# A graph layer on one Trainium2 core: TensorE's counting as a loop, and its signals sent after a drain

## The chip, the cores and the metric

The kernel runs on one core of one Trainium2 chip. The metric is the time of one execution in microseconds (us) on the device. Lower is better.

## The reference, cut to what matters

The input is `x` (12500 nodes by 256 features), and 200000 edges `src[e] -> dst[e]`, sorted by `dst`. Two graph layers run over the same edges, each followed by a residual sum and a normalization:

```
out_deg = maximum(segment_sum(ones, src), 1)
t1  = x @ W1
msg = (t1[src] + x[src] * x[dst] @ W2) / sqrt(out_deg[src]) / sqrt(out_deg[dst])
embed = where(in_cnt > 0, t1 + segment_sum(msg, dst), 0) + b0
x = layernorm(x + l2norm(leaky_relu(embed)))
xt = x @ W.T + b1
x = layernorm(x + segment_sum(xt[src], dst) / (deg + 1))
```

## The kernel before

**What flows.** Edges stand in tiles of 128; there are 1568 of them with the padding, 32 to a round, 49 rounds to a layer. For each tile GpSimd issues one indirect DMA that gathers 128 rows of a table in DRAM (1 KB each) into one slot of a ring of 32 slots in SBUF (`ring`, line 478). TensorE multiplies the slot by a 0/1 matrix of the destinations that VectorE makes (`dst_hot`), 8 tiles to a group, so 4 groups to a round; the group's sum is in a PSUM bank, and VectorE adds it to the nodes' sums (`add_group`, line 850). The table is `scaled_x` in layer 0 (x times 1/sqrt of the out degree) and `x1`, layer 0's result, in layer 1.

**What a round does on TensorE** (`round_`, lines 1105 to 1130): for each group it waits for the destinations' matrix and the bank, for each tile for the gathered rows (`rows_in`), and issues one fp32 matmul of 128x257 (two MATMUL records in the profile). The group's last matmul increments `groups_done`. For that wait VectorE, which adds the group, and ScalarE, which then copies the source numbers of the same quarter of the next round into `idx` (`refill`, line 592); GpSimd waits for that (`idx_ready`) before it gathers the quarter. Between the tiles stand the previous round's nodes, two blocks of 128: `turn_halves` after tile 19 (transposes, `halves_turned`), `products` after tile 23 (matmuls with the weights, `projected`), and in layer 0 `find_places` after tile 7 (a look-up of scale factors, `places_found`). After the last round of a layer come one more `turn_halves` and `products`. Layer 1's gathers start only when all of layer 0's rows are stored (`table1_whole`, line 369).

**Kept rows.** In layer 0, the first 6 slots of 47 rounds are not gathered in the round. Their rows are gathered from `x` ahead of the layers, while the degrees are still being counted (282 gathers, `gather_kept`, line 488), stored in DRAM by SyncE (`store_kept`, line 327), loaded again in the round, and scaled by ScalarE (line 631).

**The counting of sources**, ahead of the layers. The out degree of each node is a histogram over 12544 bins, built as 128 x 98 in PSUM. 1120 tiles are counted by one-hot matrices of VectorE (line 695), 16 tiles to a batch, 70 batches (`SRC_BATCHES`), two buffers (`hot_made`, `hot_used`). The other 448 tiles are counted by ScalarE with Sign activations (line 554), which give step functions instead, 4 tiles to a batch, 112 batches (`STEP_BATCHES`), three buffers (`steps_made`, `steps_used`). ScalarE may write batch k only when TensorE has used batch k - 3:

```
act.wait_ge(steps_used, n + 1)        # starts at 3
```

TensorE multiplies both kinds, `hist_batch` 16 matmuls (line 1035) and `step_batch` 4 matmuls (line 1042), 128x98 in bf16. The order is written out: after hist batch n come the step batches from n*112//70 to (n+1)*112//70, one or two of them, so that the last two step batches follow the last hist batch. Then VectorE takes the differences of the step sums (lines 748 to 751, after `steps_used` has reached 115), TensorE adds them to the histogram (line 1060), ScalarE and VectorE make `r` = 1/sqrt(degree), scale x with it in 14 chunks (lines 571 and 761), and ScalarE's queue stores the chunks as `scaled_x` (line 576). GpSimd starts layer 0 when all kept rows are stored (line 498) and all 14 chunks are (line 501).

Of the kernel before, what the change touches and what calls it, by code (L numbers as in the profile page):

```python
# [24 lines left out]
P = 128  # L25
# [10 lines left out]
GT = 8  # L36
GR = U // GT
GROUPS = TILES // GT
DW = D + 1
# [10 lines left out]
STEP_BATCHES = 112  # L50
STEP_TILES = STEP_BATCHES * SB
SRC_BATCHES = (TILES - STEP_TILES) // HB
# [8 lines left out]
HOTS = 4  # L61
SUMS = 2
# [8 lines left out]
UNIT = 3  # L71
# [10 lines left out]
def gnn(nc, x, src, dst, w1, w2, b0, wl, b1, out):  # L82
# [6 lines left out]
    with ExitStack() as ctx:  # L89
# [10 lines left out]
        ring = sb("ring", [P, U, PITCH])  # L100
# [12 lines left out]
        place_hot = dst_col[:, 0:KE]  # L113
# [4 lines left out]
        dst_hot = hot_space  # L118
# [5 lines left out]
        halves = sb("halves", [P, 2, 2, D])  # L124
# [3 lines left out]
        ident = sb("ident", [P, P])  # L128
# [20 lines left out]
        r = sb("r", [P, NW])  # L149
# [25 lines left out]
        def group_sum(buf):  # L175
            return banks[:, buf, 0:DW]
# [3 lines left out]
        turned = [banks[:, 4 + s, :] for s in range(2)]  # L180
        project = [banks[:, 6, s * D:(s + 1) * D] for s in range(2)]
        found = banks[:, 2:4, 0:UNIT * NW].rearrange("p b (t n) -> p b t n", t=UNIT)
# [43 lines left out]
        places_found = sem("places_found")  # L226
# [13 lines left out]
        groups_done = sem("groups_done")  # L240
# [9 lines left out]
        halves_turned = sem("halves_turned")  # L250
        projected = sem("projected")
# [24 lines left out]
        def node_no(layer, m):  # L276

            return layer * ROUNDS + m
# [739 lines left out]
        def _(pe):  # L1018
# [13 lines left out]
            def hist_batch(n, half, first, last_one):  # L1032
                pe.wait_ge(hot_made, n + 1)
                for t in range(HB):
                    last = nc.tensor.matmul(hist, lo_hot[half][:, t, :], hi_hot[half][:, t, :],  # L1035
                                            start=first and t == 0, stop=last_one and t == HB - 1)
                last.then_inc(hot_used, 1)

            def step_batch(n, third, first, last_one):
                pe.wait_ge(steps_made, n + 1)  # L1040
                for t in range(SB):
                    last = nc.tensor.matmul(step_sums, steps[:, third, t, 0:P], steps[:, third, t, P:P + HI],  # L1042
                                            start=first and t == 0, stop=last_one and t == SB - 1)
                last.then_inc(steps_used, 1)
# [5 lines left out]
            for n in range(2):  # L1050
                last = nc.tensor.transpose(banks[0:BLOCKS, n, 0:P], bounds[:, n, :], ident[:, :])
            last.then_inc(bounds_turned, 1)

            pe.wait_ge(edges_in_cols, 2)
            for n in range(SRC_BATCHES):
                hist_batch(n, n % 2, n == 0, False)
                for k in range(n * STEP_BATCHES // SRC_BATCHES, (n + 1) * STEP_BATCHES // SRC_BATCHES):
                    step_batch(k, k % 3, k == 0, k == STEP_BATCHES - 1)
            pe.wait_ge(step_diffs_made, 1)
            nc.tensor.matmul(hist, between[:, :], step_rows[1], start=False, stop=True).then_inc(counts_whole, 1)  # L1060
            pe.wait_ge(bounds_read, 1)
# [1 line left out]
            for o, half in enumerate(wl_s):  # L1063
                for k in range(KF):
                    last = nc.tensor.transpose(banks[:, 0, k * D + o * P:k * D + (o + 1) * P], half[:, k, :], ident[:, :])
# [3 lines left out]
                             start=True, stop=True).then_inc(bad_summed, 1)  # L1069
            pe.wait_ge(bases_float, 1)  # L1070
            nc.tensor.matmul(banks[:, 7, P:P + GROUPS], ones[0:1, :], base_row_f[:, 0:GROUPS],
                             start=True, stop=True).then_inc(bases_spread, 1)

            def turn_halves(layer, m):

                for s in range(2):
                    if layer == 0:
                        pe.wait_ge(mixed, 2 * m + s + 1)
                    elif s == 0:
                        pe.wait_ge(sums_taken, m + 1)  # L1080
                    for h in range(2 if layer == 0 else 1):
                        for k in range(KF):
                            place = (h * KF + k) * P
                            last = nc.tensor.transpose(turned[s][:, place:place + P], halves[:, s, h, k * P:(k + 1) * P],  # L1084
                                                       ident[:, :])
                    last.then_inc(halves_turned, 1)

            def products(layer, m):

                weights = (w1_s, w2_s) if layer == 0 else (wt_s,)  # L1090
                for s in range(2):
                    pe.wait_ge(a_ready[s], node_no(layer, m) + 1)
                    parts = [(a_t[s][:, h, k, :], w[:, k, :]) for h, w in enumerate(weights) for k in range(KF)]
                    for n, (left, right) in enumerate(parts):
                        last = nc.tensor.matmul(project[s], left, right, start=n == 0, stop=n == len(parts) - 1)  # L1095
                    last.then_inc(projected, 1)

            def find_places(i):

                pe.wait_ge(places_made, i)  # L1100
                for t in range(KEPT):
                    last = nc.tensor.matmul(found[:, t // UNIT, t % UNIT, :], place_hot[:, t * P:(t + 1) * P], r[:, :],
                                            start=True, stop=True)
                last.then_inc(places_found, 1)

            def round_(layer, i, finish, end=U, with_kept=False, find=False):

                for k in range(GR):
                    pe.wait_ge(dst_hot_made, group_no(layer, i, k) + 1)
                    pe.wait_ge(groups_added, group_no(layer, i, k) + 1)  # L1110
                    tiles = range(k * GT, min((k + 1) * GT, end))
                    for u in tiles:
                        if with_kept and u < KEPT:
                            pe.wait_ge(kept_scaled, i)
                        elif u < KEPT:
                            rounds_before = (layer * 2 + i) if layer else (0 if isinstance(i, int) and i == 0 else 1)
                            pe.wait_ge(rows_in[u], 16 * (rounds_before + 1))
                        else:
                            rounds_before = layer * (ROUNDS if u < FINAL else ROUNDS - 1) + i
                            pe.wait_ge(rows_in[u], 16 * (rounds_before + 1))  # L1120
                        last = nc.tensor.matmul(group_sum(k % SUMS), dst_hot[:, k % HOTS, u - k * GT, :], ring[:, u, 0:DW],  # L1121
                                                start=u == tiles[0], stop=u == tiles[-1])
                        if u == tiles[-1]:
                            last.then_inc(groups_done, 1)
                        if find and u == FIND_U - 1:
                            find_places(i + 1)
                        if finish and u == TURN_U - 1:
                            turn_halves(layer, i - 1)
                        if finish and u == MIX_U - 1:
                            products(layer, i - 1)  # L1130
# [6 lines left out]
            with pe.If(disordered == 0):  # L1137
                for layer in range(2):
                    first = layer == 0
# [8 lines left out]
            with pe.Else():  # L1148
                for layer in range(2):
                    with pe.Fori(0, TILES) as t:  # L1150
                        n = layer * TILES + t
# [35 lines left out]
```

## Time and profile before

| | |
|---|---|
| median of 3 runs | 3994.8 us (3993.7 to 3995.43) |
| the profiled execution | 3996.79 us, its span 3995.1 us |
| busy: TensorE, its weight loads | 2991.8 us (75%), 1828.7 us (46%) |
| busy: VectorE, ScalarE, GpSimd | 1864.8 us (47%), 664.3 us (17%), 2982.0 us (75%) |
| counting of sources | 19.8 to 295 us |
| first gather of layer 0, of layer 1, end | 374.2, 2014.7, 3995.1 us |
| granted TensorE clock, mean | 0.748 |

The shares are averages over stages. A matmul's record has a modelled end. A pause of an engine is listed with what ended it.

### The profile page before, as it was taken

The page shows a single profiled execution, that of the slowest core. Times are in us where ns is not written, and L with a number is a line of the kernel's source. Part 1 is how long each engine was busy: PE and PEld are TensorE (multiplying, and loading weights), DVE is VectorE, ACT ScalarE, POOL GpSimd, SP SyncE. Part 2 cuts the span into 40 slices and gives each one's busy share as a digit, 9 for nine tenths or more (in the row PEclk, how much of TensorE's full clock was granted, in tenths as well). Part 3 has the DMA queues.
Part 4 walks back from the last instruction along what each step waited for, and adds up shares of the span by engine and source line. Part 5 has one row for each costly group of instructions (what it writes and reads, how often), then busy time and mean ns, then how long its engine had stood idle before and what let it go on. Part 6 is the DMA issues. An engine that isn't in the chain of part 4 may idle for free.

```text
span 3995.1 us, 42771 instructions
## 1 busy us (share of the span) xinstructions
PE 2991.8 (75%) x10186; PEld 1828.7 (46%) x10186; DVE 1864.8 (47%) x3536; ACT 664.3 (17%) x2054; POOL 2982.0 (75%) x3146
## 2 busy tenths in 40 slices
PE   4551777777777777777777877888888888878887
PEld 4441555555555555555433333344334343334443
DVE  9994555555555555555423333333333323232323
ACT  7992111111111111111100000000000000000000
POOL 7776777777777777777667777777777777777776
PEclk5555888988888888888867777666766666776667
DMA  8878455555555555555334443434443434343433
GB/s 256 272 233 309 150 156 155 155 156 155 156 155 155 156 158 156 158 155 156 116 94 118 117 118 116 119 115 120 115 120 115 120 115 120 115 121 114 120 115 107
DMA packets 294217, 582.43 MB, mean 146 GB/s; under 512 B 60723, under 2 KB 176100, under 8 KB 294180
## 3 DMA queue, kind: packets, MB, share of 16 engines
q0 software_dynamic: 150048, 409.93, 35.4%
q1 hardware_dynamic: 131364, 159.19, 11.9%
q10 hardware_dynamic: 12768, 12.85, 0.9%
q8 instruction: 20, 0.33, 0.0%
q14 instruction: 17, 0.14, 0.0%
HBM read 506.27 MB, written 75.45 MB: 146 GB/s over the span
## 4 chain that ended last, share of the span: by engine, by line
POOL 65%; issue 23%; POOLq 1%; PE 1%; DVE 0%; DVEq 0%; DMA 0%; ACT 0%; SPq 0%; ACTq 0%
POOL ring L478 65%; PE banks L1095 0%; POOLq L511 0%; DVEq L688 0%; POOLq L475 0%; PE banks L1121 0%; POOLq L476 0%; PE banks L1084 0%; DMA ring<-scaled_x,idx 0%; DMA ring<-x,idx 0%; POOL ring L488 0%; DMA x<-out_t 0%; DVE stats L917 0%; DVE out_t L929 0%; DVE big L850 0%
## 5 line engine op out<-in xcount | busy, mean ns | idle before, releaser
L1121 PE MATMUL banks<-ring,hot_space 128*128 128x257 f32 x6252 | 2470.7, 521 | 806.8 <-DMA ring<-x,idx 330.9
L1121 PEld LDWEIGHTS banks<-ring,hot_space 128*128 128x128 f32 x6252 | 1309.8, 242 | 1896.2 <-DMA ring<-x,idx 1058.0
L478 POOL DMA_INDIRECT ring<-x,idx x1563 | 1486.9, 951 | 505.3 <-issue 475.9
L478 POOL DMA_INDIRECT ring<-scaled_x,idx x1281 | 1221.2, 953 | 402.7 <-issue 402.7
L850 DVE SCALAR_TENSOR_TENSOR big<-banks,here_mask,big 128x257 f32 x784 | 343.9, 480 | 1604.5 <-PE banks L1121 1604.3
L806 DVE TENSOR_TENSOR hot_space<-banks,dst_rel 128x1024 f32<-128x1024 f32 x395 | 483.5, 1225 | 212.6 <-issue 210.8
L592 ACT COPY idx<-src_col 128x8 int32 (+1 forms) x392 | 77.3, 197 | 2145.7 <-PE banks L1121 2145.7
L488 POOL DMA_INDIRECT ring<-in_x,src_col x276 | 264.1, 957 | 84.1 <-issue 84.1
L554 ACT ACTIVATE dst_rel<-columns,halves 128x128 bf16<-128x128 f32 (+1 forms) x896 | 253.5, 374 | 23.8 <-PE banks L1042 19.6
L1035 PE MATMUL banks<-hot_space 128*128 128x98 bf16 x1120 | 104.2, 283 | 139.2 <-DVE hot_space L695 139.2
L1095 PE MATMUL banks<-w_s,a_t 128*128 128x256 f32 x784 | 179.3, 383 | 0.0
L1095 PEld LDWEIGHTS banks<-w_s,a_t 128*128 128x128 f32 x784 | 150.7, 192 | 20.8 <-ACT a_t L614 0.4
L1035 PEld LDWEIGHTS banks<-hot_space 128*128 128x128 bf16 x1120 | 89.2, 141 | 154.2 <-DVE hot_space L695 144.8
L695 DVE TENSOR_TENSOR hot_space<-banks,src_lo 128x2048 bf16<-128x2048 f32 x70 | 159.8, 2282 | 0.1
L695 DVE TENSOR_TENSOR hot_space<-banks,src_hi 128x1568 bf16<-128x1568 f32 x70 | 124.7, 1782 | 0.0
L614 ACT COPY a_t<-banks 128x512 f32<-128x512 f32 (+1 forms) x196 | 88.1, 480 | 219.5 <-PE banks L1084 219.0
L631 ACT ACTIVATE ring<-ring,r_kept 128x256 f32<-128x256 f32 x282 | 117.6, 495 | 22.4 <-issue 22.4
L1084 PE MATMUL banks<-ident,halves 128*128 128x128 f32 x588 | 108.6, 334 | 12.3 <-DVE halves L862 8.5
L1084 PEld LDWEIGHTS banks<-ident,halves 128*128 128x128 f32 x588 | 94.2, 178 | 34.4 <-DVE halves L862 10.8
L874 DVE SCALAR_TENSOR_TENSOR e<-banks,scal,b_s 128x256 f32<-128x256 f32 x98 | 42.9, 479 | 124.8 <-PE banks L1095 124.8
L1095 PE MATMUL banks<-wt_s,a_t 128*128 128x256 f32 x392 | 95.4, 388 | 0.1
L622 ACT ACTIVATE scal<-mv,epsilon 128x2 f32<-128x2 f32 x98 | 29.0, 295 | 370.2 <-DVEq L688 370.2
(115 smaller groups left out, 1193.2 us busy)
## 6 DMA issues: line engine op xcount, KB each, us to landing
kept_rows<-ring SPq DMA_DIRECT2D x94, 384.0 KB, 3.4
ring<-kept_rows SPq DMA_DIRECT2D x47, 768.0 KB, 5.5
ring<-x,idx POOLq DMA_INDIRECT x1563, 2.8
ring<-scaled_x,idx POOLq DMA_INDIRECT x1281, 2.8
dst_col<-in_src SPq DMA_DIRECT2D x47, 384.0 KB, 5.8
scaled_x<-big ACTq DMA_DIRECT2D x14, 896.0 KB, 17.5
x<-out_t SPq DMA_DIRECT2D x98, 128.0 KB, 2.4
x_t<-x SPq DMA_DIRECT2D x98, 128.0 KB, 2.3
```

The source lines that it names most:

```text
L478: g.indirect_dma_start(ring[:, u, 0:D], None, table[layer], bass.IndirectOffsetOnAxis(ap=idx[:, u:u + 1], axis=0)).then_inc(rows_in[u], 16)
L488: g.indirect_dma_start(early[place][:, t * D:(t + 1) * D], None, x, bass.IndirectOffsetOnAxis(ap=sources, axis=0)).then_inc(early_in[place ...
L554: last = nc.scalar.activation(steps[:, third, t, first:first + size], columns[:, 0:size], ACT.Sign, bias=step_digits[:, digit, bass.ds(n * ...
L614: nc.scalar.copy(a_t[s][:, 0:parts, :, :].rearrange("p h k n -> p (h k n)"), turned[s][:, 0:parts * D]).then_inc(a_ready[s], 1)
L631: last = nc.scalar.activation(ring[:, u, 0:D], ring[:, u, 0:D], ACT.Copy, scale=r_kept[:, bass.ds(i * KEPT + u, 1)])
L695: last = nc.vector.tensor_tensor(hots[half], lane_row[:, 0:size].unsqueeze(1).to_broadcast([P, HB, size]), vals.unsqueeze(2).to_broadcast( ...
L806: nc.vector.tensor_tensor(dst_hot[:, buf, :, :], lane_row.unsqueeze(1).to_broadcast([P, GT, P]), rel, ALU.is_equal).then_inc(dst_hot_made, 1)
L850: last = nc.vector.scalar_tensor_tensor(here, group_sum(k % SUMS), here_mask[:, n, bass.ds(i * GR + k, 1)], here, ALU.mult, ALU.add)
L1035: last = nc.tensor.matmul(hist, lo_hot[half][:, t, :], hi_hot[half][:, t, :], start=first and t == 0, stop=last_one and t == HB - 1)
L1084: last = nc.tensor.transpose(turned[s][:, place:place + P], halves[:, s, h, k * P:(k + 1) * P], ident[:, :])
L1095: last = nc.tensor.matmul(project[s], left, right, start=n == 0, stop=n == len(parts) - 1)
L1121: last = nc.tensor.matmul(group_sum(k % SUMS), dst_hot[:, k % HOTS, u - k * GT, :], ring[:, u, 0:DW], start=u == tiles[0], stop=u == tiles ...
```

## The change

It concerns TensorE's program alone. First, the counting is a loop. A "span" is two hist batches and three step batches: hist, step, step, hist, step. One span stands ahead of the loop and 34 in it, with waits on register values; 35 spans hold all 70 hist batches and 105 of the 112 step batches. The last 7 step batches stand behind the loop, one after the other. Second, in `turn_halves`, `products`, `find_places` and `round_` the increment no longer hangs on the last matmul: the engine drains and then increments by an instruction of its own.

```
-            for n in range(SRC_BATCHES):
-                hist_batch(n, n % 2, n == 0, False)
-                for k in range(n * STEP_BATCHES // SRC_BATCHES, (n + 1) * STEP_BATCHES // SRC_BATCHES):
-                    step_batch(k, k % 3, k == 0, k == STEP_BATCHES - 1)
+            def span(n, first):
+                for half in range(2):
+                    hist_batch(2 * n + half, half, first and half == 0, False)
+                    for third in ((0, 1), (2,))[half]:
+                        step_batch(3 * n + third, third, first and third == 0, False)
+
+            span(0, True)
+            with pe.Fori(1, SRC_BATCHES // 2) as n:
+                span(n, False)
+            for k in range(SRC_BATCHES // 2 * 3, STEP_BATCHES):
+                step_batch(k, k % 3, False, k == STEP_BATCHES - 1)
...
-                    last.then_inc(halves_turned, 1)
+                    pe.drain()
+                    pe.sem_inc(halves_turned, 1)
...
-                    last.then_inc(projected, 1)
+                    pe.drain()
+                    pe.sem_inc(projected, 1)
...
-                last.then_inc(places_found, 1)
+                pe.drain()
+                pe.sem_inc(places_found, 1)
...
                         if u == tiles[-1]:
-                            last.then_inc(groups_done, 1)
+                            pe.drain()
+                            pe.sem_inc(groups_done, 1)
```

How TensorE's instructions stand at the end of the counting, before (L1035 is a hist batch, L1042 a row of step batches at 4 matmuls each, L1060 adds the steps' differences, L1065 transposes a weight):

```order
L1035 MATMUL banks<-hot_space 128x98 x16
L1042 MATMUL banks<-dst_rel 128x98 x4
L1035 MATMUL banks<-hot_space 128x98 x16
L1042 MATMUL banks<-dst_rel 128x98 x8
L1035 MATMUL banks<-hot_space 128x98 x16
L1042 MATMUL banks<-dst_rel 128x98 x8
L1060 MATMUL banks<-e,between 128x98
L1065 MATMUL banks<-ident,a_t 128x128 x4
```

The same place now, from the loop's first row to the weight's transposes (`REGISTER_ALU` and `ISA` are the registers' work for the waits and the loop; L1068 and L1073 are what L1060 and L1065 were):

```order
L1035 MATMUL banks<-hot_space 128x98 x16
L1040 ISA
L1042 MATMUL banks<-dst_rel 128x98 x4
L1040 REGISTER_ALU
L1042 MATMUL banks<-dst_rel 128x98 x4
L1033 REGISTER_ALU
L1035 MATMUL banks<-hot_space 128x98 x16
L1040 REGISTER_ALU
L1042 MATMUL banks<-dst_rel 128x98 x4
L1063 REGISTER_ALU
L1063 COMPARE_AND_BRANCH
L1042 MATMUL banks<-dst_rel 128x98 x28
```

Where 2 step batches (8 matmuls) stood behind the last hist batch, 1 stands in the loop's last pass and 7 (28 matmuls) behind it. The order of the two layers' matmuls is the same as before; drains and increments have no row in these lists.

## Rows read from the trace of the kernel before

**Rows 1.** The page, chain that ended last, shares by engine.

```profile
POOL 65%; issue 23%; POOLq 1%; PE 1%; DVE 0%; DVEq 0%; DMA 0%; ACT 0%; SPq 0%; ACTq 0%
```

**Rows 2.** The page, groups: busy, mean ns, idle before.

```profile
L478 POOL DMA_INDIRECT ring<-scaled_x,idx x1281 | 1221.2, 953 | 402.7 <-issue 402.7
```

**Rows 3.** Windows, a layer each: PE, PEld, DVE, ACT, POOL busy, PEclk, DMA share, GB/s.

```profile
600.00:1800.00 1200.00, 895.01 (x3663) 678.80 (x3662) 690.68 (x1505) 201.81 (x552) 909.35 (x955) 0.88 0.51 156
2400.00:3600.00 1200.00, 995.74 (x2272) 479.61 (x2271) 376.84 (x778) 71.88 (x239) 909.08 (x956) 0.69 0.41 117
```

**Rows 4.** Waits in one round of layer 0, 1146 to 1178.6 us.

```profile
PE banks L1121 <- DMA ring<-scaled_x,idx: 4.6, 7, 1.2
PE banks L1121 <- ACT ring L631: 3.5, 1, 3.5
```

**Rows 5.** Timeline of ScalarE: the second refill of a round.

```profile
1151.63 0.20 ACT L592 COPY idx<-src_col 128x8 int32 x1 [6.04 <-PE banks L1121]
```

**Rows 6.** Timeline of TensorE: 8 tiles in a row, one tile alone.

```profile
1179.95 3.66 PE L1121 MATMUL banks<-ring,hot_space 128*128 128x257 f32 x16
1184.54 0.67 PE L1121 MATMUL banks<-ring,hot_space 128*128 128x257 f32 x2 [0.93 <-DMA ring<-scaled_x,idx]
```

**Rows 7.** The page, DMA issues: count, median us to landing.

```profile
ring<-scaled_x,idx POOLq DMA_INDIRECT x1281, 2.8
```

**Rows 8.** Chain between counting and layer 0: start us, us, what.

```profile
361.45 10.44 issue
371.89 0.04 POOLq L501
```

**Rows 9.** Timeline of ScalarE at the same place.

```profile
370.90 1.69 ACT L585 COPY big<-zeros 128x1792 f32<-128x1792 f32 x1 [1.65 <-DMA scaled_x<-big]
```

**Rows 10.** Timeline of both layers' ends.

```profile
1987.66 0.88 DVE L874 SCALAR_TENSOR_TENSOR e<-banks,scal,b_s 128x256 f32<-128x256 f32 x2 [2.56 <-PE banks L1095]
...
2005.12 0.88 DVE L874 SCALAR_TENSOR_TENSOR e<-banks,scal,b_s 128x256 f32<-128x256 f32 x2 [7.09 <-PE banks L1095]
...
2014.68 0.94 POOL L478 DMA_INDIRECT ring<-x,idx  x1 [29.41 <-SPq L369]
...
3989.07 0.88 DVE L900 SCALAR_TENSOR_TENSOR out_t<-banks,scal,e 128x256 f32<-128x256 f32 x2 [1.20 <-PE banks L1095]
```

**Rows 11.** Timeline of 283 to 295 us, the counting's end.

```profile
283.02 6.82 ACT L554 ACTIVATE dst_rel<-columns,halves 128x128 bf16<-128x128 f32 x24 [0.41 <-PE banks L1042]
...
290.07 0.86 PE L1042 MATMUL banks<-dst_rel 128*128 128x98 bf16 x8
...
290.74 2.34 ACT L554 ACTIVATE dst_rel<-columns,halves 128x128 bf16<-128x128 f32 x8 [0.90 <-PE banks L1042]
...
292.68 1.49 PE L1035 MATMUL banks<-hot_space 128*128 128x98 bf16 x16 [1.75 <-DVE hot_space L695]
...
293.97 0.85 PE L1042 MATMUL banks<-dst_rel 128*128 128x98 bf16 x8
...
294.86 0.26 DVE L748 COPY e<-banks 128x98 f32<-128x98 f32 x1 [1.65 <-PE banks L1042]
```

**Rows 12.** Waits of 2400 to 3600 us: TensorE's pauses without a releaser.

```profile
PEld banks L1121 <- issue: 52.0, 59, 1.2
```

**Rows 13.** Timeline of ScalarE's queue: the first store of scaled_x.

```profile
304.38 0.39 ACTq L576 DMA_DIRECT2D scaled_x<-big  x1
```

**Rows 14.** DMA queues, 304 to 361.5 us: packets, MB, share of 16 engines.

```profile
q10 hardware_dynamic: 11379, 11.46, 57.7%
q0 software_dynamic: 1992, 5.47, 23.8%
q1 hardware_dynamic: 1916, 5.16, 23.7%
```

**Rows 15.** DMA queues, 361.5 to 372 us.

```profile
q10 hardware_dynamic: 1389, 1.39, 37.5%
```

**Rows 16.** Timeline of TensorE: 8 tiles in a row at the lower clock.

```profile
420.27 6.70 PE L1121 MATMUL banks<-ring,hot_space 128*128 128x257 f32 x16 [3.21 <-ACT ring L631]
```

More of the change, by code:

```diff
@@ L1083, in turn_halves @@
                             place = (h * KF + k) * P
-                            last = nc.tensor.transpose(turned[s][:, place:place + P], halves[:, s, h, k * P:(k + 1) * P],
-                                                       ident[:, :])
-                    last.then_inc(halves_turned, 1)
+                            nc.tensor.transpose(turned[s][:, place:place + P], halves[:, s, h, k * P:(k + 1) * P],
+                                                ident[:, :])
+                    pe.drain()
+                    pe.sem_inc(halves_turned, 1)
             def products(layer, m):
@@ L1094, in products @@
                     for n, (left, right) in enumerate(parts):
-                        last = nc.tensor.matmul(project[s], left, right, start=n == 0, stop=n == len(parts) - 1)
-                    last.then_inc(projected, 1)
+                        nc.tensor.matmul(project[s], left, right, start=n == 0, stop=n == len(parts) - 1)
+                    pe.drain()
+                    pe.sem_inc(projected, 1)
             def find_places(i):
@@ L1101, in find_places @@
                 for t in range(KEPT):
-                    last = nc.tensor.matmul(found[:, t // UNIT, t % UNIT, :], place_hot[:, t * P:(t + 1) * P], r[:, :],
+                    nc.tensor.matmul(found[:, t // UNIT, t % UNIT, :], place_hot[:, t * P:(t + 1) * P], r[:, :],
                                             start=True, stop=True)
-                last.then_inc(places_found, 1)
+                pe.drain()
+                pe.sem_inc(places_found, 1)
             def round_(layer, i, finish, end=U, with_kept=False, find=False):
@@ L1120, in round_ @@
                             pe.wait_ge(rows_in[u], 16 * (rounds_before + 1))
-                        last = nc.tensor.matmul(group_sum(k % SUMS), dst_hot[:, k % HOTS, u - k * GT, :], ring[:, u, 0:DW],
+                        nc.tensor.matmul(group_sum(k % SUMS), dst_hot[:, k % HOTS, u - k * GT, :], ring[:, u, 0:DW],
                                                 start=u == tiles[0], stop=u == tiles[-1])
                         if u == tiles[-1]:
-                            last.then_inc(groups_done, 1)
+                            pe.drain()
+                            pe.sem_inc(groups_done, 1)
                         if find and u == FIND_U - 1:
```

## The prediction

> **What bounds the kernel now.** I read first the chain that ended last. It is GpSimd with 65% and "issue" with 23% [rows 1], and the groups say what that is, in layer 0 1281 gathers of 0.953 us with 402.7/1281 = 0.31 us before each [rows 2], so one gather each 1.26 us. The reader should see that the pause before a gather has no releaser other than issue: in the rounds GpSimd waits for nobody. Then the windows: in 1200 us GpSimd is busy 909 us in either layer, while TensorE has 895 us in layer 0 and 996 us in layer 1 [rows 3]. TensorE is the second load, not the bound. The waits of one round of layer 0 say what it has in hand: of 32.6 us (26 gathers) it waits 4.6 us for gathered rows and 3.5 us for ScalarE's scaling [rows 4], 8.1 us together. A late TensorE reaches GpSimd only through `idx`, and there is more room: ScalarE refilled the round's second quarter at 1151.8 us [rows 5], while TensorE waited for tile 16 until 1184.5 us [rows 6], 2.8 us after its gather was issued [rows 7]. Tile 16 was thus issued at about 1181.7 us and tile 8, the first of that quarter, eight gathers earlier, at about 1171.7 us: 20 us of room.
>
> So the end is set where GpSimd does wait, and at the two ends of layers. Between counting and layer 0 it waits 10.44 us, until 371.89 us [rows 8]. The last chunk of `scaled_x` had landed by 370.9 us, when ScalarE starts to zero its place [rows 9], so the last 1.0 us belongs to the last kept store. At the end of layer 0 it waits 29.41 us for the stored rows [rows 10], and behind the last gather of layer 1 stands a similar tail.
>
> **The loop.** Its registers and branch come to six rows for two hist batches. TensorE waits 1.75 us for VectorE before a hist batch [rows 11], and VectorE has a second buffer; the bound from above for a turn of a loop is the 1.2 us that is the longest pause without a releaser in the rounds, which are a loop already [rows 12]. It is hidden: 0 us. Should a turn cost over 1.75 us, the second buffer is next to cover it.
>
> The step batches are what changes. A span uses 3 for 2 hist batches, before it was 3.2. ScalarE makes one in 6.82/3 = 2.27 us when nothing holds it [rows 11], and a span has two periods of VectorE, 2 x 3.9 = 7.8 us (292.68 less 288.78), for 3 x 2.27 = 6.8 us. It was held by the buffers already (0.41 and 0.90 us before its last pieces); now it is held more, and cannot use the time to run ahead by more than three. Now the end. Before, ScalarE starts the last step batch at 290.74 us, when TensorE has freed a buffer behind the last but one hist batch, and TensorE is done with all at 293.97 + 0.85 = 294.82 us [rows 11]. In the changed order the same moment frees the buffer for step batch 105, and behind it stand 105 to 111, seven batches: 290.74 + 7 x 2.27 = 306.6, and TensorE's four matmuls 0.4 to 0.5 us more, 307.1 us. The counting ends **12.3 us later**.
>
> What that costs: `r`, the scaling and the stores of `scaled_x` all shift; the first store was issued at 304.38 us [rows 13] and goes to 316.7 us. But the stores are bound by the DMA engines and shared with the kept rows, whose gathers end at 361.45 us as before. From 304.38 to 361.5 us the stores' queue q10 moved 11.46 MB, 0.201 MB a us, beside 5.47 and 5.16 MB of the two others [rows 14], and 1.39 MB were left for the time after [rows 15]. With the later start it moves 44.8 x 0.201 = 9.0 MB by then and leaves 3.86 MB, 2.47 MB more. GpSimd issues no gathers after 361.45 us, so the engines are the stores': all three queues together moved 22.1 MB in 57.5 us, 0.384 MB a us, and q10 alone had 57.7% of the engines for its 11.46 MB, which is 0.345 at 100%. 2.47 MB take 6.4 us by the one, 7.2 us by the other. I take 6.6: the last chunk lands at 377.5 instead of 370.9 us, GpSimd goes on at 377.5 instead of 371.9, **+5.6 us**. Bounds: 0 (the 1.0 us of slack and full cover) and +11.3 (no cover: 370.9 + 12.3).
>
> "Issuing engines are not separate DMA queues" in the Trainium skill's page DMA: Bandwidth & Descriptors says that transfers of all queues run on the same 16 engines and interleave; by it the stores take over what the gathers leave, as taken here. The rows agree so far that the three queues' shares sum to about 105% of the engines.
>
> **The drains.** Each round has 4 for groups, 2 for transposes, 2 for products, in layer 0 also one for the look-up: 9 and 8. No drain of TensorE is in the trace. Nearest is the difference between tiles in a row, 3.66/8 = 0.46 us, and a tile alone, 0.67 us [rows 6]: 0.21 us to fill and empty, which a drain exposes when work stands behind it. The drain and the increment are queue instructions; one such on GpSimd takes 0.04 us [rows 8], two 0.08. So 0.3 us where TensorE has work behind it, 0.1 us on a signal alone. From below 0; from above nothing shows it, and I use twice, 0.6.
>
> In the rounds: 9 x 0.3 = 2.7 us against 8.1 us of waiting, and behind that the 20 us of `idx`. Hidden, 0 us. Without that cover it would be 47 x 2.7 = 127 us. In the tails they lie on the path. Layer 0's last round, up to VectorE's work at 1987.66 us [rows 10]: two transposes' drains, a group's, the first product's, 4 x 0.3, and the last product's signal, 0.1: 1.3 us. Then up to 2005.12 us [rows 10] one 0.3 and one 0.1; the transposes' are covered by ScalarE's clearing of the sums. Layer 1, up to 3989.07 us [rows 10]: a group's signal, a transposes' signal, and 0.3 + 0.1 for products, 0.6. Sum **2.3 us**, bounds 0 and 5.
>
> The Trainium skill's page TensorE: Matmul & The Clock Gate, "Single matmul latency", gives about 175 ns by which a lone matmul exceeds its columns' time, and in "Step-by-step" that a stream hides it; this speaks against the change, and the 0.21 us of the rows are near it. By its figure the sum of the tails would be an estimated 2.1 us.
>
> **Sum.** 5.6 + 2.3 = 7.9 us. The profiled execution took 3996.79 us, 1.7 above its span and 2.0 above the median of 3994.8; it would come to 4004.7, the median to 4002.7. A measurement of this kernel can tell 0.2% or 8.0 us from no change, so this forecast lies just inside the bound, as a small loss.
>
> **The rivals.**
>
> *Slower, the stores don't speed up.* If q10 keeps its 0.201 MB a us after the gathers end, 3.86 MB take 19.2 us: 380.7, +8.8 us; with the tails +11.1, 4005.9 us. With no cover at all +11.3 + 2.3, 4008.4. It decides from a rate under about 0.33 MB a us. For it: a queue alone at full rate is nowhere in the trace. Against: q10's share of 57.7% grows when others stop.
>
> *Hidden.* The last step batches come sooner than I have them, or the kept stores end the wait in any case; only the tails are left: +2.3, 3997.1 us. For it: 1.0 us of slack is there. Against: 12.3 us is far more than that.
>
> *Slower, dear drains.* If a drain costs more than 8.1/9 = 0.9 us, TensorE can't follow in layer 0: at 1.0 us it is 9 x 0.1 x 46 = 41 us more, 4044 us. Against: a tile alone ends after 0.67 us in all.
>
> *Slower, the clock.* The granted clock was 0.88 in layer 0, so about a quarter of the time at 1.2 GHz [rows 3]. At that level 8 tiles take 6.70 us [rows 16] against 3.66 [rows 6], 32 tiles 26.8 against 14.6 us. If drains kept it there, a round's tiles alone would grow by 12.2 us, over the 8.1 in hand: 4 us x 46 = +190, 4190 us. Against: a TensorE that falls behind no longer waits for rows, and the clock comes back; GpSimd sets how much it has to do in a us. The page of the clock gate says in "HAM oscillation" that pauses between bursts throttle the engine, which is this rival's mechanism.
>
> **How the numbers follow.** Forecast 0.60; stores that don't speed up 0.20; hidden 0.12; drains 0.03 and clock 0.03; faster for a reason I don't see 0.02. The forecast's own range is 3999.5 to 4006, and since its middle is at the bound, I give 0.25 of its 0.60 to slower. Slower: 0.25 + 0.20 + 0.06 = 0.51; faster 0.03; within 0.46. The range: from 3997 (hidden) to 4012 (no cover, tails at their upper bound).
>
> **What would show it.** Step batches at the counting's end: 7 pieces of 4 matmuls, 2.27 us apart, to 307 us. First gather of layer 0 at 379.8 instead of 374.2. Rounds of 32.6 and 40.2 us as before, GpSimd's pauses 0.3 us. Pauses of 0.2 to 0.3 us on TensorE behind products and transposes. From layer 0's last gather to layer 1's first 1.7 us more, and 0.6 at the end. It is wrong if GpSimd waits within a round, if the first gather moves by under 3 or over 8 us, or if layers change their length by more than 3 us.

## The result and the profile after

The changed kernel takes **4011.52 us** (median of 6 runs, 4010.28 to 4013.43) against 3995.01 us of the kernel before in as many runs beside it. The ratio is 1.0041 (95% interval 1.0031 to 1.0051), so it is slower by 16.5 us. The profiled spans are 4010.5 and 3995.1 us, 15.4 us apart, and this is where they part:

| stretch | before, us | after, us | difference |
|---|---|---|---|
| start to the first gather of layer 0 | 374.2 | 380.1 | +5.9 |
| first to last gather of layer 0 | 1610.1 | 1621.6 | +11.5 |
| last gather of layer 0 to the first of layer 1 | 30.4 | 31.5 | +1.2 |
| first to last gather of layer 1 | 1961.8 | 1958.0 | -3.8 |
| last gather to the end | 18.6 | 19.2 | +0.7 |

**The start.** Timeline of the counting's end, TensorE, ScalarE and VectorE, of the changed kernel; it answers to [rows 11] and [rows 13]:

```profile
291.11 15.75 ACT L554 ACTIVATE dst_rel<-columns,halves 128x128 bf16<-128x128 f32 x56 [0.98 <-PE banks L1042]
...
304.68 0.51 PE L1042 MATMUL banks<-dst_rel 128*128 128x98 bf16 x4 [1.73 <-ACT dst_rel L554]
...
306.92 0.51 PE L1042 MATMUL banks<-dst_rel 128*128 128x98 bf16 x4 [1.73 <-ACT dst_rel L554]
307.46 0.26 DVE L748 COPY e<-banks 128x98 f32<-128x98 f32 x1 [13.94 <-PE banks L1042]
316.98 0.39 ACTq L576 DMA_DIRECT2D scaled_x<-big  x1
```

ScalarE makes its last 7 batches (56 activations, 8 to a batch) without a stop. TensorE takes one every 2.24 us and waits 1.73 us before each. VectorE goes on at 307.46 instead of 294.86 us, the first store is at 316.98 instead of 304.38: 12.6 us later, both. The first fence below has q10, the stores' queue, from 304 to 361.5 us (against [rows 14]: 11.46 MB), the second from 361.5 to 380 us (against [rows 15]: 1.39 MB); columns: packets, MB, share of 16 engines.

```profile
q10 hardware_dynamic: 8989, 9.05, 46.1%
```

```profile
q10 hardware_dynamic: 3779, 3.80, 59.1%
```

Chain that ended last, at the same place: the last store lands at 378.2 us, and GpSimd passes its wait; then the first gather on GpSimd's timeline (both answer to [rows 8]):

```profile
366.63 11.57 DMA scaled_x<-big
...
378.40 0.51 POOLq L503
```

```profile
380.08 0.94 POOL L478 DMA_INDIRECT ring<-scaled_x,idx  x1 [18.25 <-issue]
```

**The layers.** The page's groups of gathers (busy us, mean ns, idle before and its releaser):

```profile
L478 POOL DMA_INDIRECT ring<-x,idx x1563 | 1483.2, 949 | 506.4 <-issue 475.8
L478 POOL DMA_INDIRECT ring<-scaled_x,idx x1281 | 1232.7, 962 | 408.1 <-issue 407.5
```

Against [rows 2] the 1281 gathers of layer 0 are busy for 1232.7 instead of 1221.2 us. The idle time before them, less 12.76 and 18.25 us before the first, is 389.9 both times. In both profiles no pause before a gather within a layer is over 0.32 us. So GpSimd waits for nobody in the rounds, as before, and the 11.5 us are in the gathers' own length. In layer 1 they are shorter, 1483.2 against 1486.9 us. The windows (columns as in [rows 3]) show no slower TensorE clock, 0.90 and 0.74 against 0.88 and 0.69:

```profile
600.00:1800.00 1200.00, 927.01 (x3646) 665.34 (x3645) 686.63 (x1487) 198.47 (x545) 911.78 (x947) 0.90 0.51 155
2400.00:3600.00 1200.00, 943.64 (x2275) 463.72 (x2276) 379.41 (x775) 73.23 (x239) 908.50 (x958) 0.74 0.40 118
```

**What a drain costs TensorE.** Timeline of the changed kernel, TensorE's weight loads and matmuls of `products` in one round:

```profile
1169.77 1.59 PEld L1104 LDWEIGHTS banks<-w_s,a_t 128*128 128x128 f32 x8 [0.48 <-issue]
1169.78 4.06 PE L1104 MATMUL banks<-w_s,a_t 128*128 128x256 f32 x16
...
1171.84 1.59 PEld L1104 LDWEIGHTS banks<-w_s,a_t 128*128 128x128 f32 x8 [0.48 <-issue]
```

Each half's loads begin 0.48 us after the loads of the half before ended; between the two halves stand one drain and one increment. The whole piece took 3.62 us before and takes 4.06 (the median of 49 such pieces in either kernel).

**Layers' ends**, timeline, answering to [rows 10]:

```profile
2005.68 0.88 DVE L874 SCALAR_TENSOR_TENSOR e<-banks,scal,b_s 128x256 f32<-128x256 f32 x2 [3.25 <-PEq L1105]
...
2023.69 0.88 DVE L874 SCALAR_TENSOR_TENSOR e<-banks,scal,b_s 128x256 f32<-128x256 f32 x2 [7.65 <-PEq L1105]
...
2033.24 0.94 POOL L478 DMA_INDIRECT ring<-x,idx  x1 [30.61 <-SPq L369]
```

30.61 us between the layers against 29.41; with the 0.7 us at the end the tails cost 1.9 us.

**Why gathers got longer.** A plain gather takes 0.946 us. In layer 0, 72 of 1281 were over 0.962 us before and 171 are now; what they have over 0.946 sums to 10.1 and 21.2 us (counts and sums here and below are worked out from the trace's records of gathers and of VectorE's instructions). Here is one of them in the changed kernel, with VectorE beside it, and the same instruction of the kernel before, both from timelines:

```profile
1140.80 0.94 POOL L478 DMA_INDIRECT ring<-scaled_x,idx  x1 [0.30 <-issue]
1142.05 1.07 POOL L478 DMA_INDIRECT ring<-scaled_x,idx  x1 [0.30 <-issue]
```

```profile
1141.88 0.76 DVE L878 SCALAR_TENSOR_TENSOR e<-e 128x256 f32<-128x256 f32 x2
```

```profile
1162.97 0.95 POOL L478 DMA_INDIRECT ring<-scaled_x,idx  x1 [0.30 <-issue]
1164.23 0.95 POOL L478 DMA_INDIRECT ring<-scaled_x,idx  x1 [0.30 <-issue]
```

```profile
1163.38 0.76 DVE L878 SCALAR_TENSOR_TENSOR e<-e 128x256 f32<-128x256 f32 x2
```

After, the first of L878's two instructions of about 0.42 us is running when the gather at 1142.05 starts, and ends 0.25 us after that start; the gather takes 0.12 us more. Before, L878 lay between the starts of two gathers and both took 0.95. For 308 of the 351 long gathers of the two profiles, the surplus is what remains of VectorE's instruction at the gather's start, less 0.13 us, to within 0.01 us. Only some instructions do it: those with two inputs in SBUF (L860, L862, L878, L895, L913) and some with a single one in SBUF (L813, L815, L929, all three of them `TENSOR_SCALAR`). L850, L874 and L900, which read PSUM, run over gathers' starts and hold none; nor does L917, which has a single input in SBUF. Who began first matters as well: 50 times one of the holding lines, with over 0.15 us to go, had begun less than 0.12 us ahead of the gather, and the gather kept its length.

42 of the other 43 long gathers are lengthened in a second way. Here L806, which holds nobody, runs at the gather's start, and L813 begins 0.35 us behind it:

```profile
1151.39 1.22 DVE L806 TENSOR_TENSOR hot_space<-banks,dst_rel 128x1024 f32<-128x1024 f32 x1 [1.58 <-issue]
1152.18 1.01 POOL L478 DMA_INDIRECT ring<-scaled_x,idx  x1 [0.30 <-issue]
1152.53 0.55 DVE L813 TENSOR_SCALAR dst_col<-dst_col 128x768 int32<-128x768 int32 x1
```

The gather ends at 1153.19 us, 0.11 us after L813's end at 1153.08. All 42 look like this: L813 begins 0.31 to 0.37 us after the gather, and the gather ends 0.12 us after L813. There are 4 of them in the kernel before, for 0.3 us, and 38 in the changed one, for 2.2 us. So the step to 21.2 us is 5.7 us of L878, 2.9 us of L813 and L815 running at the start, 1.9 us of L813 begun later, and 0.6 us of L860 and L862.

So my theory for the rounds was: **a drain delays TensorE's signal, the signal moves VectorE's work by some tenths of a us against GpSimd's raster of 1.25 us, and more of it falls on the moments at which a gather can be held.** The rivals: late TensorE work reaches GpSimd in another way (through `idx`, or the order of the DMAs); or the loop has to do with it.

### The profile page after: what moved, and what is told of

Same layout as the page of the kernel before. It is cut to its first block, busy times and chain, and to the rows that moved or that the text cites. A ratio compares the mean times of both kernels' runs of the same rounds, so it can differ in the third digit from the quotient of the medians.

```text
span 4010.5 us, 43841 instructions
## 1 busy us (share of the span) xinstructions
PE 2967.2 (74%) x10186; PEld 1787.7 (45%) x10186; DVE 1871.8 (47%) x3536; ACT 665.3 (17%) x2054; POOL 2990.2 (75%) x3146
## 4 chain that ended last, share of the span: by engine, by line
POOL 64%; issue 24%; DVE 6%; ACTq 1%; DMA 1%; PEld 1%; POOLq 1%; ACT 1%; DVEq 1%; PEldq 0%; SPq 0%; PE 0%
POOL ring L478 64%; DVE hot_space L695 6%; ACTq L576 1%; PEld banks L1132 0%; DVEq L688 0%; DMA ring<-scaled_x,idx 0%; DMA scaled_x<-big 0%; POOLq L511 0%; ACT dst_rel L554 0%; PEldq L1135 0%; ACT big L571 0%; POOLq L475 0%; PEldq L1105 0%; PEld banks L1104 0%; DVEq L733 0%
## 5 line engine op out<-in xcount | busy, mean ns | idle before, releaser
L1132 PE MATMUL banks<-ring,hot_space 128*128 128x257 f32 x6252 | 2325.1, 504 | 796.2 <-DMA ring<-x,idx 356.9
L478 POOL DMA_INDIRECT ring<-x,idx x1563 | 1483.2, 949 | 506.4 <-issue 475.8
L478 POOL DMA_INDIRECT ring<-scaled_x,idx x1281 | 1232.7, 962 | 408.1 <-issue 407.5
L850 DVE SCALAR_TENSOR_TENSOR big<-banks,here_mask,big 128x257 f32 x784 | 343.6, 480 | 1564.6 <-PEq L1135 1564.6
L806 DVE TENSOR_TENSOR hot_space<-banks,dst_rel 128x1024 f32<-128x1024 f32 x395 | 483.4, 1224 | 216.6 <-issue 213.8
L1035 PE MATMUL banks<-hot_space 128*128 128x98 bf16 x1120 | 104.2, 282 | 141.2 <-DVE hot_space L695 141.2
L1104 PE MATMUL banks<-w_s,a_t 128*128 128x256 f32 x784 | 196.6, 394 | 7.9
L1104 PEld LDWEIGHTS banks<-w_s,a_t 128*128 128x128 f32 x784 | 141.9, 191 | 62.7 <-issue 46.6
L1035 PEld LDWEIGHTS banks<-hot_space 128*128 128x128 bf16 x1120 | 89.2, 141 | 156.2 <-DVE hot_space L695 146.8
L1092 PE MATMUL banks<-ident,halves 128*128 128x128 f32 x588 | 125.1, 329 | 25.5 <-DVE halves L862 10.2
L1104 PE MATMUL banks<-wt_s,a_t 128*128 128x256 f32 x392 | 114.2, 415 | 13.9 <-issue 9.7
L874 DVE SCALAR_TENSOR_TENSOR e<-banks,scal,b_s 128x256 f32<-128x256 f32 x98 | 42.9, 479 | 158.3 <-PEq L1105 158.3
L1092 PEld LDWEIGHTS banks<-ident,halves 128*128 128x128 f32 x588 | 82.2, 167 | 76.9 <-issue 43.0
L1104 PEld LDWEIGHTS banks<-wt_s,a_t 128*128 128x128 f32 x392 | 68.6, 195 | 62.8 <-issue 56.7
## 6 DMA issues: line engine op xcount, KB each, us to landing
scaled_x<-big ACTq DMA_DIRECT2D x14, 896.0 KB, 16.5
```

The costliest lines, as they stand in the source:

```text
L478: g.indirect_dma_start(ring[:, u, 0:D], None, table[layer], bass.IndirectOffsetOnAxis(ap=idx[:, u:u + 1], axis=0)).then_inc(rows_in[u], 16)
L806: nc.vector.tensor_tensor(dst_hot[:, buf, :, :], lane_row.unsqueeze(1).to_broadcast([P, GT, P]), rel, ALU.is_equal).then_inc(dst_hot_made, 1)
L850: last = nc.vector.scalar_tensor_tensor(here, group_sum(k % SUMS), here_mask[:, n, bass.ds(i * GR + k, 1)], here, ALU.mult, ALU.add)
```

## The experiments

Short diffs are against the kernel before unless another is named. The same counts for all profiled kernels: long gathers and their surplus in us, in layer 0 with the share of VectorE's lines (named by their numbers in the kernel before), and in layer 1. "L813 later" is the second way, L813 begun after the gather's start. The plain gather is 946 ns, in the rows with * 949.

| kernel | layer 0 | of it L813, L815 | L813 later | L860, L862 | L878 | L913 | layer 1 |
|---|---|---|---|---|---|---|---|
| before | 72, 10.1 | 3.2 | 0.3 | 5.7 | 0.6 | 0.2 | 69, 8.9 |
| changed | 171, 21.2 | 6.1 | 2.2 | 6.3 | 6.3 | under 0.2 | 39, 5.6 |
| changed, again* | 171, 20.6 | 6.5 | 2.1 | 5.4 | 6.3 | 0.2 | 41, 5.4 |
| drains alone | 158, 22.0 | 5.5 | 2.2 | 6.5 | 7.2 | 0.3 | 51, 6.9 |
| loop and order alone | 74, 9.9 | 2.5 | 0.2 | 6.1 | 0.8 | 0.4 | 69, 9.0 |
| order alone* | 83, 10.5 | 2.8 | 0.1 | 6.9 | under 0.2 | 0.3 | 67, 8.4 |
| drain in `products` alone | 130, 17.3 | 1.2 | 0.5 | 5.7 | 7.0 | 2.5 | 75, 9.0 |
| drains of groups alone | 141, 18.5 | 2.2 | 0.3 | 6.3 | 6.8 | 2.6 | 66, 9.6 |
| drain in `turn_halves` alone | 80, 11.0 | 2.2 | 0.3 | 6.8 | 0.8 | 0.5 | 53, 5.7 |
| drain in `find_places` alone* | 80, 10.3 | 2.4 | 0.4 | 6.8 | 0.3 | 0.2 | 63, 7.7 |
| changed, two copies ahead of L874 | 110, 11.3 | 0.9 | 0.2 | 5.3 | 2.5 | 2.3 | 45, 6.5 |
| changed, one copy | 107, 16.7 | 2.2 | 2.0 | 6.3 | 0.2 | under 0.2 | 51, 6.7 |
| before, bias in PSUM | 87, 11.0 | 3.6 | 0.4 | 5.9 | 0.7 | 0.3 | 8, 0.6 |
| changed, bias in PSUM | 165, 20.6 | 6.0 | 2.5 | 4.9 | 6.9 | 0.2 | 8, 0.6 |

### Drains alone, loop and order alone

Drains alone: all four drains, the counting as before.

```
-                    last.then_inc(projected, 1)
+                    pe.drain()
+                    pe.sem_inc(projected, 1)
```

and so in the three other places.

> The kernel before with all four kinds of drain and the counting unrolled in its old order. Theory A (collisions): the drains move VectorE's work against GpSimd's gathers, and gathers that coincide with certain VectorE instructions take longer; so this run has the changed kernel's gather time in layer 0, 1232.7 us busy against 1221.2, with no shift of the first gather: it starts at 374.2 us, and the kernel takes 9 to 11 us more than before, about 4005. Theory B (the later start does it: the counting moves something in time and the layers' gathers suffer from that): gathers stay at 1221 us, only the tails' 2 us are left, about 3997.

Loop and order alone: the first hunk of the change, and no drain.

> The changed kernel's counting alone, no drains. Theory A: first gather at 380.1 us, 5.9 later than before, gathers of layer 0 at about 1221 us busy, 4001 us in all. Theory B: first gather at 380.1 and gathers at about 1233 us, 4010 us.

Measured, beside 3996.94 us of the kernel before: drains alone 4008.75 (ratio 1.0028, 1.0018 to 1.0039), +11.8 us; loop and order 4002.73 (1.0015, 1.0005 to 1.0024), +5.8 us. Page of the drains alone, then of loop and order alone:

```profile
L478 POOL DMA_INDIRECT ring<-scaled_x,idx x1281 | 1233.6, 963 | 402.8 <-issue 401.6
```

```profile
L478 POOL DMA_INDIRECT ring<-scaled_x,idx x1281 | 1220.9, 953 | 408.0 <-issue 408.0
```

The first gather is at 374.30 us with the drains alone and at 379.79 with loop and order alone. The two parts add up within their intervals: 11.8 + 5.8 = 17.6 against 16.5 us for the change. With loop and order alone the gathers keep their 1220.9 us, so the loop has nothing to do with the rounds.

### Order alone

Against the changed kernel, with the drains undone too:

```
-            with pe.Fori(1, SRC_BATCHES // 2) as n:
+            for n in range(1, SRC_BATCHES // 2):
```

> The changed order of the counting, three step batches to two hist batches and seven at the end, written out without a loop, and no drains. If the order alone makes the delay: first gather at 379.8 to 380.1 us as with the loop, 7 pieces of step batches at the end. If the loop's turns or its register waits have a part in it: the first gather comes before 379 us.

One run, 4010.97 us, on a chip where the kernel before takes 4003.9 (19 runs). The first gather is at 380.37 us; in the one run with the drain in `find_places` alone, on the same chip, it is at 374.63: +5.7 us without any loop, against 374.2 to 379.8 with it. So the whole 5.7 to 5.9 us come with the order, that is the seven step batches at the end; the loop's registers and branches cost nothing that shows.

### One kind of drain at a time

Each of these has one of the four drains, in the kernel before.

> The kernel before with drains behind the products alone. Theory A: VectorE's L878 and L881, which follow the products, are most of the new collisions (1 and 6 of 94 gathers hit before, 43 and 88 in the changed kernel), while L813 and L815, which follow a group, are as before (4 and 23 of 47): about half of the 11.5 us, so 5 to 7 us, about 4001. If each kind only adds its own small delay and the collisions need all of them, under 2 us, 3997. Theory B: nothing, under 1 us.

> The kernel before with drains at the groups' ends alone. Theory A: L813, L815 and L819 move into the gathers (38, 41 and 45 hits of 47 in the changed kernel against 4, 23 and 25), L878 and L881 stay out of them: 3 to 6 us, about 4000. Theory B: under 1 us.

> The kernel before with a drain behind the transposes alone. Theory A: it delays the second block's transposes and the products by about 0.3 us or less, and VectorE's work on the products with them; L878 would start at 0.6 instead of 0.3 and 0.7 us after a gather's start, 1.0 for its second half, just ahead of the point where it holds the next gather. Layer 0's gathers 1 to 7 us over before's, less than with drains at the products or groups.

> The kernel before with a drain behind the look-up alone. Theory A: its signal is awaited by VectorE's L826, which stands between a group's matrices and its sum; it delays little, so layer 0's gathers are within 3 us of 1221 us busy.

| drain alone in | median, us | before beside it | ratio (95%) | gathers of layer 0, busy us |
|---|---|---|---|---|
| `products` | 4004.56 | 3996.94 | 1.0020 (1.0010 to 1.0029) | 1228.8 |
| groups | 4004.97 | 3996.94 | 1.0020 (1.0011 to 1.0030) | 1230.1 |
| `turn_halves` | 3993.63, one run | 3996.69 | | 1221.9 |
| `find_places` | 4004.83, one run | 4003.9 | | 1224.9 (plain 949) |

The four are not a sum: `products` and groups give 7.6 and 8.0 us each and all together 11.8. A cost of the drains themselves would add up. The table above fits with that: each of the two alone brings L878 onto gathers' starts (0.6 to 7.0 and 6.8 us), which can happen only once. I had looked for the groups' drains to show in L813 and L815, VectorE's work in front of a group; they didn't (3.2 before, 2.2). The groups' drains delay the products behind them as well, which would move the same L878, and L913 behind it; this link wasn't tested by itself. The 5.5 us of L813 and L815 come only with several drains together. For drains in `turn_halves` alone I had expected 1 to 7 us more in layer 0's gathers; the one run shows 0.7, no cost in all, and in layer 1 L895 partly off the starts (layer 1's surplus 8.9 to 5.7 us). For `find_places` the one run shows no cost either.

### Moving VectorE by hand

If only the position counts, more delay on the changed kernel should give time back. In `finish_sums`, layer 0, ahead of L874, two copies that nobody reads:

```
                     v.wait_ge(projected, 2 * m + 4)
+                    for n in (P, P // 8):
+                        nc.vector.tensor_copy(columns[:, 0:n], lane_row[:, 0:n])
+                        ordered()
```

> The changed kernel, with two small copies and drains, some 0.5 us of extra work, in VectorE's queue ahead of its work on layer 0's products (L874 and what follows). Nothing is left out. Theory A (a gather is held when it needs the port at about 0.1 us after its start while L878 runs): more work on VectorE puts L878 back between these moments, its about 44 held gathers in layer 0 fall below 10, and the gathers' busy time of layer 0 falls from 1232.7 us by 5 to 6 us, if the later work (L860 to L862, L813, L815) is not moved into them more than it is now; the kernel is faster than the changed one by 3 to 6 us. Rival C (TensorE's drains slow the gathers directly, or VectorE's load as such does): the gathers stay at 1232 us or get longer, 4011 us or more.

Timeline of VectorE: the copies delay the next instruction by 0.73 us.

```profile
1169.11 0.54 DVE L874 COPY columns<-banks 128x128 f32<-128x128 f32 x2 [3.13 <-PEq L1108]
1169.84 0.88 DVE L877 SCALAR_TENSOR_TENSOR e<-banks,scal,b_s 128x256 f32<-128x256 f32 x2 [0.19 <-issue]
```

Median 4012.3 us of 10 runs (4005.0 to 4015.58) beside 4003.9: ratio 1.0021 (1.0011 to 1.0030), where the change has 1.0041 (1.0031 to 1.0051), and in a second set of runs 1.0043 (1.0026 to 1.0060). The sets were not run side by side. Its page:

```profile
L478 POOL DMA_INDIRECT ring<-scaled_x,idx x1281 | 1222.6, 954 | 408.6 <-issue 405.2
```

The profiled execution is the quickest of the ten, 4005.0. The 3.4 us that "issue" leaves open are 11 of the usual pauses of 0.3 us, put down to `idx`; none is over 0.31 us. With more work on VectorE in every round, the gathers of layer 0 are 10.1 us shorter than in the changed kernel. A theory in which lateness costs time would have them longer. L878 was freed only in part, though: I had expected fewer than 10 held gathers, 20 were left, and L913 came to hold 40 for 2.3 us.

The same with one copy, 0.38 us, to see whether L878 alone can be moved, next to the changed kernel on the same chip:

```
+                    nc.vector.tensor_copy(columns[:, :], lane_row)
+                    ordered()
```

> The changed kernel with one copy and drain, some 0.45 us, in VectorE's queue ahead of its work on layer 0's products; the last try had two and moved L878 by 0.73 us, which freed L878 in half its cases and brought L913 into the gathers instead. Theory A: L878 stands 0.11 to 0.27 us after a gather's start in the changed kernel and 0.3 to 0.5 us in the one before, where it holds nobody; by 0.45 us later it is there again. Held gathers at L878 from 44 to under 5, L913's stay under 10, layer 0's gathers about 1226 us busy, 6 us faster than the changed kernel here. Rival C: more work on VectorE, no gain.

> The changed kernel, unaltered, on the same chip as the next two, since a comparison with it across chips is uncertain by some us. Gathers of layer 0 at 1232 us busy (or that much more than before by 11 us, if this chip's gathers all take some ns longer), 16 us slower than before.

One copy: 4008.79 us (5 runs; 1.0034, 1.0020 to 1.0048); the changed kernel again: 4013.45 us (4 runs; 1.0043, 1.0026 to 1.0060), beside 3996.69. The medians differ by 4.7 us and the surplus by 20.6 - 16.7 = 3.9, but the intervals overlap, so the times alone don't settle it. The records do: of the 6.3 us of L878, 0.2 are left, and L881 behind it, which held one gather for 0.1 us in the changed kernel, now holds 36 gathers for 5.7 us. The copy moved the clash by one instruction, which I had not expected. L815 lost 4.0 of its 6.0 us. This run also shows the clash from the other side, in 28 of the 47 rounds that have an L813:

```profile
658.69 0.95 POOL L478 DMA_INDIRECT ring<-scaled_x,idx  x1 [0.30 <-issue]
659.25 0.77 DVE L813 TENSOR_SCALAR dst_col<-dst_col 128x768 int32<-128x768 int32 x1
```

L813, begun 0.54 to 0.60 us after the gather, takes 0.73 to 0.79 instead of 0.55 us, and the gather keeps its 0.95. Begun 0.34 to 0.53 us after the gather (13 times in this run), L813 keeps its length and the gather ends 0.12 us after it. So around that moment one of the two holds the other, and which one is settled by when L813 begins.

### Taking a holder away

L895 of layer 1 reads a bias and `x_t`, both in SBUF, and in the kernel before its instructions run over 46 gathers' starts and hold 45 for 6.9 us. A copy of the bias in PSUM makes it an instruction with one input in PSUM, at the same length and place:

```
+            nc.vector.tensor_copy(banks[:, 7, P:P + D], b1_s[:, :])
+            ordered()
...
-                        nc.vector.scalar_tensor_tensor(e[s][:, :], b1_s[:, :], scal[:, 4 + s:5 + s], x_t[s][:, :],
+                        nc.vector.scalar_tensor_tensor(e[s][:, :], banks[:, 7, P:P + D], scal[:, 4 + s:5 + s], x_t[s][:, :],
```

> The kernel before, with one operand of layer 1's L895 (the bias) read from PSUM instead of SBUF, so that the instruction has one SBUF input instead of two; its time on VectorE is the same. Theory A, with the holder being what has two SBUF inputs: the 45 held gathers at L895 vanish, layer 1's gathers fall from 1486.9 to about 1480 us busy, 7 us faster than before, about 3990 (before at 3997 in the last comparison). Rival D (it is the moment alone that matters, whatever VectorE reads): no change, 1487 us.

Timelines of GpSimd and VectorE in one round of layer 1, of the kernel before and then with the bias in PSUM:

```profile
2089.68 1.12 POOL L478 DMA_INDIRECT ring<-x,idx  x1 [0.30 <-issue]
```

```profile
2089.10 0.88 DVE L895 SCALAR_TENSOR_TENSOR e<-b_s,scal,x_t 128x256 f32<-128x256 f32 x2
```

```profile
2090.25 0.95 POOL L478 DMA_INDIRECT ring<-x,idx  x1 [0.30 <-issue]
```

```profile
2089.66 0.88 DVE L895 SCALAR_TENSOR_TENSOR e<-banks,scal,x_t 128x256 f32<-128x256 f32 x2
```

Both times L895 still has about 0.3 us to go when the gather starts (2089.10 + 0.88 - 2089.68 = 0.30; 2089.66 + 0.88 - 2090.25 = 0.29), and only with both inputs in SBUF is the gather longer, by 0.30 - 0.13 = 0.17 us. The page:

```profile
L478 POOL DMA_INDIRECT ring<-x,idx x1563 | 1478.1, 946 | 504.7 <-issue 475.7
```

No gather is held by L895 any more. The kernel takes 3997.1 us (10 runs) beside 4003.9: ratio 0.9984 (0.9974 to 0.9993), 6.8 us faster, as its 6.9 us say. So it is **faster than the kernel before**, and with that than the changed one.

The same edit on the changed kernel:

> The changed kernel with the bias of layer 1's L895 in PSUM. Theory A: of its 28 held gathers at L895 none is left, 4.8 us less in layer 1's gathers (1483.2 to about 1478), 5 us faster than the changed kernel here. Layer 0 as in the changed kernel.

4006.64 us (8 runs; ratio 1.0026, 1.0015 to 1.0037), 6.8 us under the changed kernel's 4013.45 on this chip; the gathers of layer 1 went from 1487.5 to 1478.6 us, layer 0 kept its surplus (20.6 us both). The 6.8 us are more than L895's 4.6 and the 4.8 of layer 1's whole surplus, but the changed kernel has only 4 runs here (4011.31 to 4019.58) and the two intervals overlap, so the rest stays open.

## Why the prediction was right and wrong

The measured +16.5 us is about twice the predicted +7.9, inside the range of 3997 to 4012, and on the side that had the largest chance, slower. The size was wrong because a term was missing.

- **The counting's end: right.** 12.6 us later against 12.3, by the mechanism given: seven batches at ScalarE's pace, 2.24 us apart against 2.27. The stores: 9.05 MB by 361.5 us against 9.0 predicted, 3.80 MB left against 3.86, and the last landed at 378.2 against 377.5 us. The extra 2.41 MB took 378.2 - 370.9 = 7.3 us, 0.33 MB a us, so they sped up, and the rival in which they keep their 0.201 MB a us is out. +5.9 us against +5.6.
- **The loop: right.** It costs nothing that shows; the order alone, without a loop, gave +5.7 us (one run).
- **The tails: right in size.** +1.9 us against +2.3.
- **A drain's price: too low.** 0.48 us up to the next weight load, and 0.44 us more for the piece of 16 matmuls, where I took 0.3; both are inside the bound of 0.6. TensorE had the room for it, and what its later signals did is the next point.
- **"In the rounds ... Hidden, 0 us": this step failed.** That GpSimd would wait for nobody was right, and no round contains a wait. What I concluded from it, that the rounds keep their length, was not. The step treated a gather's 0.953 us [rows 2] as a constant, though a plain one is 0.946 and the mean already held 10.1 us of surplus. A later signal from TensorE moves VectorE's instructions, and some of these lengthen the gathers that they meet: +11.5 us in layer 0, of which 11.1 are surplus. In layer 1 the same surplus fell by 3.3 us and the layer by 3.8. The text's own test, layers that change their length by more than 3 us, says so.
- **The rivals.** Dear drains would have shown as GpSimd waiting; no pause of GpSimd in the rounds is over 0.31 us. The clock went up rather than down. 4011.5 us lies above the stores that don't speed up (4005.9) and above those without any cover (4008.4), and far below dear drains (4044): no rival had this mechanism, and the range held the time only through bounds that stood for other causes, by luck. (The chances have a slip too: "faster" is 0.02 in the list and 0.03 in the sum.)

The Trainium skill's page SBUF — State Buffer, section "SBUF: two separate sides", describes GpSimd and VectorE as sharing a port pair that one of them locks for a whole instruction, VectorE when it runs in a two-port mode or, against a GpSimd instruction that reads SBUF, has two SBUF inputs. The trace agrees on which instructions hold a gather: two SBUF inputs, and none of L850, L874 and L900 with an input in PSUM; L895 changed from one kind to the other by its bias alone (45 held to none). Whether L813, L815 and L929 run in a two-port mode no view shows. The trace doesn't agree that a gather would keep the ports for its whole length: L813, begun 0.31 to 0.37 us into a gather, ran its usual 0.55 us and held the gather 42 times.

What stays open: that L878's and L815's surplus in the changed kernel would vanish if one of their inputs were in PSUM wasn't tried; for them the evidence is the fit of the long gathers and the runs with copies. Why the drains together, and not one alone, bring L815 onto the starts wasn't taken apart either. That layer 1's gain comes from the drains in `turn_halves` rests on one run.

## What to carry to other kernels

When an engine works at its own steady pace and seems to wait for nobody, compare its mean instruction with its plain one before calling it a constant: if a part of them is longer, another engine's work is in their way, and any shift of that work moves the time, up or down, by more than the shift's own cost. Take such a clash away by changing the instruction (an input in PSUM), rather than by moving it: here each delay handed part of it to another line, and any later edit can move it back. And when a producer with few buffers is paired with a consumer in a fixed order, batches left for the end run at the producer's pace with the consumer idle.

## What the runs showed of the hardware

- A gather of 128 rows takes GpSimd 0.946 us. One of VectorE's holding instructions that is already running when it starts lengthens it by what remains of that instruction less 0.13 us (308 gathers of two profiles, to within 0.01 us), but 50 such instructions that began less than 0.12 us ahead of it held none.
- L813 holds a gather also when it begins after the gather's start: begun 0.31 to 0.37 us after it (42 gathers of the two profiles), the gather ends 0.12 us after L813. Begun 0.54 to 0.60 us after it (28 times in the run with one copy), it is L813 that is lengthened, from 0.55 us to 0.73 to 0.79. L878's second instruction at 1142.3 us, 0.25 us after a gather's start, ends within it and holds nothing.
- Some instructions with a single SBUF input hold too: L929 in layer 1 (2.0 us before), L813 and L815. And L881 held 36 gathers when a copy had moved it onto their starts.
- The plain gather took 946 ns in eleven profiles and 949 in three. 3 ns by 2844 gathers are 8.5 us; on the chip where the kernel before takes 4003.9 us, the profile of the bias in PSUM has 946 ns and its execution took 3987.94 us, where its nine other executions took 3996.34 to 3998.88. Both lengths occur on that chip. Two profiles should be compared with that number beside them. What sets it stays open.
- A drain and an increment of TensorE between two pieces of work cost 0.48 us up to the next weight load, and the piece of 16 matmuls with one inside went from 3.62 to 4.06 us.
- The granted clock rose with the drains (0.748 to 0.777 in the mean of the profiled executions; 0.776 with the drains alone, 0.740 with loop and order alone), though they put more pauses into TensorE's work.
